# An LSTM with a residual: the sums of a step in two banks by halves of the features, matmuls of 256 columns

## The reference

```python
xW = einsum('ntd,dg->ntg', x, Wx) + b          # x: (32, 512, 512), Wx: (512, 2048)
def step(carry, xw_t):                          # 512 steps, batch 32, 512 features
    a = xw_t + prev_h @ Wh                      # Wh: (512, 2048)
    i, f, o = sigmoid(a[:, :3 * 512]) in thirds
    g = tanh(a[:, 3 * 512:])
    next_c = f * prev_c + i * g
    next_h = o * tanh(next_c)
return x + hs                                   # all hidden states, plus x
```

## Time and profile before

| | |
|---|---|
| median of 3 runs | 2726.16 us (2726.15 to 2726.85) |
| the profiled execution | 2726.29 us |
| its span, first to last instruction | 2724.5 us |
| matmuls, and as many weight loads | 49152 |
| mean granted clock of TensorE | 0.989 |

### The profile page before, as it was taken

One profiled execution on the slowest core, in us unless ns is written; L12 is line 12 of the kernel. 1 busy time (PEld: TensorE's weight loads), 2 busy tenths in 40 slices (PEclk: granted clock), 3 DMA queues, 4 the chain that ended last, 5 costly groups with the idle time before them and its releaser, 6 DMA issues.

```text
span 2724.5 us, 121148 instructions
## 1 busy us (share of the span) xinstructions
PE 2671.2 (98%) x49152; PEld 1387.0 (51%) x49152; DVE 1929.8 (71%) x8121; ACT 1245.7 (46%) x3722; POOL 45.9 (2%) x134
## 2 busy tenths in 40 slices
PE   3999999999999999999999999999999999999998
PEld 0455555555555555555555555555555555555554
DVE  6777777777777777777777777777777777777776
ACT  3444444444444444444444444444444444444444
POOL 0000000000000000000000000000000000000000
PEclk6999999999999999999999999999999999999999
DMA  6111111111111111111111111111111111111111
GB/s 144 37 43 35 38 38 40 35 39 42 35 38 38 40 35 39 42 35 38 38 39 35 39 42 35 39 38 39 35 39 42 35 39 39 38 35 39 42 36 26
DMA packets 223520, 109.94 MB, mean 40 GB/s; under 512 B 25216, under 2 KB 222464, under 8 KB 222464
## 3 DMA queue, kind: packets, MB, share of 16 engines
q1 hardware_dynamic: 223488, 109.48, 15.7%
HBM read 75.83 MB, written 33.55 MB: 40 GB/s over the span
## 4 chain that ended last, share of the span: by engine, by line
PE 97%; issue 1%; DVE 1%; DMA 1%; SPq 0%; ACT 0%; POOL 0%; DVEq 0%; POOLq 0%
PE Z L244 97%; DMA wx_raw<-in_Wx 1%; DVE wh_lo L435 0%; SPq L213 0%; SPq L200 0%; DVE wmax L417 0%; SPq L208 0%; DVE h_hi L475 0%; ACT tanh_c L356 0%; POOL wmax_all L537 0%; DVE xmax L396 0%; DVE x_lo L381 0%; DVE zs L407 0%; DVE c L490 0%; DVE scales L410 0%
## 5 line engine op out<-in xcount | busy, mean ns | idle before, releaser
L350 ACT ACTIVATE act<-Z,scales 128x192 f32<-128x192 f32 x1022 | 430.9, 422 | 1159.5 <-PE Z L244 1159.5
L244 PE MATMUL Z<-wx_hi,x_hi 128*32 128x512 f16 x8176 | 807.7, 379 | 9.3 <-DVE x_lo L381 9.3
L244 PE MATMUL Z<-wh_hi,hT_hi 128*32 128x512 f16 x8176 | 808.1, 379 | 8.0 <-DVE hT_hi L480 8.0
L244 PE MATMUL Z<-wh_lo,hT_hi 128*32 128x512 f16 x8176 | 808.1, 379 | 0.0
L244 PE MATMUL Z<-wx_hi,x_lo 128*32 128x512 f16 x8176 | 807.6, 379 | 0.0
L244 PE MATMUL Z<-wx_lo,x_hi 128*32 128x512 f16 x8176 | 807.6, 379 | 0.0
L244 PE MATMUL Z<-wh_hi,hT_lo 128*32 128x512 f16 x8176 | 533.1, 379 | 0.0
L486 DVE TENSOR_TENSOR fc<-act,c 128x64 f32<-128x64 f32 x512 | 115.3, 225 | 570.2 <-ACT act L350 570.2
L356 ACT ACTIVATE tanh_c<-c 128x64 f32<-128x64 f32 x1024 | 262.3, 256 | 269.7 <-DVE c L497 249.2
L475 DVE SCALAR_TENSOR_TENSOR h_hi<-act,scales,tanh_c 128x64 f16<-128x64 f32 x1024 | 291.3, 285 | 113.1 <-ACT tanh_c L356 86.3
L327 ACT ACTIVATE Z<-bias_bc,scales 128x512 f32<-128x512 f32 x511 | 344.6, 674 | 0.0
(11 more groups left out here) (50 smaller groups left out, 1286.1 us busy)
## 6 DMA issues: line engine op xcount, KB each, us to landing
x_in<-in_x SPq DMA_DIRECT2D x512, 64.0 KB, 2.0
x_res<-in_x SPq DMA_DIRECT2D x512, 64.0 KB, 2.1
out_y<-y SPq DMA_DIRECT2D x512, 64.0 KB, 1.7
wx_raw<-in_Wx SPq DMA_DIRECT2D x16, 256.0 KB, 8.8
wh_raw<-in_Wh SPq DMA_DIRECT2D x16, 256.0 KB, 19.0
bias_bc<-in_bias SPq DMA_DIRECT2D x4, 64.0 KB, 2.0
h_in<-in_h SPq DMA_DIRECT2D x4, 16.0 KB, 13.8
```

The lines of the kernel that those rows point to most:

```text
L244: return nc.tensor.matmul(bank[L * j:L * j + B, :], lhsT, rhs, start=False, stop=last, skip_group_check=True)
L350: nc.scalar.activation(half_gates(act, a)[:, 0:3], half_gates(Z[s], a)[:, 0:3], ACT.Sigmoid, scale=scale).then_inc(sig_done, 1)
```

## The change

A step's Z now takes two banks, one for each half of the features (a = 0, 1), with 256 columns in each: four gates of 64 features. Steps t and t+2 share a pair of banks, side by side in each bank. Every matmul of 512 columns becomes two of 256, with the same stationary operand loaded for each. The weights, `act` and the bias are laid out by halves (tile, half, gate, 64). In the recurrent part the low part of h comes last as before, but now all chunks for half 0 and then all for half 1, with a `z_done` after each; ScalarE waits for each half by itself. The bias is loaded by eight DMAs, the low parts of the weights are cut by gate and no longer by tile.

```diff
-        def bank(name):
-            return ctx.enter_context(nc.psum_tensor(name, [P, 512], F32))
+        def bank_pair(name):
+            return ctx.enter_context(nc.psum_tensor(name, [P, 2, 512], F32))
...
-        Z = [bank(f"Z{s}") for s in range(TB)]
+
+        Z = [bank_pair(f"Z{q}") for q in range(2)]
...
+        HW = ZW // 2
...
+        def gate(tile, a, g, n=1):
+            return tile[:, a * HW + g * HC:a * HW + (g + n) * HC]
+
+        def both_halves(tile, g):
+            return tile.rearrange("p (a g c) -> p g a c", a=2, g=4)[:, g]
+
+        def z_half(s, a, g=0, n=4):
+            at = s // 2 * HW
+            return Z[s % 2][:, a, at + g * HC:at + (g + n) * HC]
+
+        def by_half(w, j, a):
+            at = j * C + a * HC
+            return w.rearrange("p (g c) -> p g c", g=4)[:, :, at:at + HC]
+
+        def by_halves(w):
+            return w.rearrange("p (g k c) -> p k g c", g=4, c=HC)
+
+        def as_halves(w):
+            return w.rearrange("p (k g c) -> p k g c", g=4, c=HC)
+
+        def halves_of_gate(w, g):
+            return w.rearrange("p (k g c) -> p g k c", g=4, c=HC)[:, g]
+
+        def gate_by_halves(w, g):
+            return w[:, g * NJ * C:(g + 1) * NJ * C].rearrange("p (k c) -> p k c", c=HC)
...
             for j in range(NJ):
-                sp.dma_start(bias_bc[L * j:L * j + B].rearrange("p (g c) -> p g c", g=4),
-                             bias_view[j].partition_broadcast(B)).then_inc(bias_loaded, 16)
+                for a in range(2):
+                    sp.dma_start(bias_bc[L * j:L * j + B, a * HW:(a + 1) * HW].rearrange("p (g c) -> p g c", g=4),
+                                 bias_view[j, :, a * HC:(a + 1) * HC].partition_broadcast(B)).then_inc(bias_loaded, 16)
...
-            def add(bank, j, lhsT, rhs, last=False):
-
-                return nc.tensor.matmul(bank[L * j:L * j + B, :], lhsT, rhs, start=False, stop=last, skip_group_check=True)
+            def add(s, a, j, lhsT, rhs, last=False):
+
+                return nc.tensor.matmul(z_half(s, a)[L * j:L * j + B], lhsT, rhs, start=False, stop=last, skip_group_check=True)
...
-            for s in range(TB):
-                for j in range(NJ):
-                    mm = nc.tensor.matmul(Z[s][L * j:L * j + B, :], x_T[:, 0, 0, :],
-                                          x_in[:, 0].rearrange("p t c -> p (t c)"), start=True, stop=True)
-                mm.then_inc(banks_opened, 1)
+            for q in range(2):
+                for a in range(2):
+                    for j in range(NJ):
+                        mm = nc.tensor.matmul(Z[q][L * j:L * j + B, a], x_T[:, 0, 0, :],
+                                              x_in[:, 0].rearrange("p t c -> p (t c)"), start=True, stop=True)
+                    mm.then_inc(banks_opened, 1)
...
-                raw = by_tile(wx_raw[:, ch])
-                for j in range(NJ):
-                    add(Z[0], j, x_T[:, ch, 0, :], raw[:, j])
+                for a in range(2):
+                    for j in range(NJ):
+                        add(0, a, j, x_T[:, ch, 0, :], by_half(wx_raw[:, ch], j, a))
...
+            def columns(w, ch, j, a):
+                return w[:, ch, j * ZW + a * HW:j * ZW + (a + 1) * HW]
...
                     for xp, wp in ((x_hi, wx_hi), (x_hi, wx_lo), (x_lo, wx_hi)):
+                        for a in range(2):
+                            for j in range(NJ):
+                                mm = add(s, a, j, xp[:, r, ch, s * B:(s + 1) * B], columns(wp, ch, j, a))
+                mm.then_inc(xpart_done, 1)
+
+            def recurrent_part(t, s):
+                for ch in range(NCH):
+                    if ch % 2 == 0:
+                        pe.wait_ge(hT_hi_done, 2 * t - 1 + ch // 2)
+                    for w in (wh_hi, wh_lo):
+                        for a in range(2):
+                            for j in range(NJ):
+                                add(s, a, j, hT_hi[:, ch, :], columns(w, ch, j, a))
+                pe.wait_ge(hT_lo_done, t)
+
+                for a in range(2):
+                    for ch in range(NCH):
                         for j in range(NJ):
-                            mm = add(Z[s], j, xp[:, r, ch, s * B:(s + 1) * B], wp[:, ch, j * ZW:(j + 1) * ZW])
-                mm.then_inc(xpart_done, 1)
-
-            def recurrent_part(t, s):
-                for part, ht in enumerate((hT_hi, hT_lo)):
-                    for ch in range(NCH):
-                        if part == 0 and ch % 2 == 0:
-                            pe.wait_ge(hT_hi_done, 2 * t - 1 + ch // 2)
-                        if part == 1 and ch == 0:
-                            pe.wait_ge(hT_lo_done, t)
-                        for w in ((wh_hi, wh_lo) if part == 0 else (wh_hi,)):
-                            for j in range(NJ):
-                                mm = add(Z[s], j, ht[:, ch, :], w[:, ch, j * ZW:(j + 1) * ZW], part == 1 and ch == NCH - 1)
-                mm.then_inc(z_done, 1)
+                            mm = add(s, a, j, hT_lo[:, ch, :], columns(wh_hi, ch, j, a), ch == NCH - 1)
+                    mm.then_inc(z_done, 1)
...
-                nc.scalar.activation(Z[s][:, :], bias_bc[:, :], ACT.Copy, scale=scale).then_inc(bias_placed, 1)
-
-            sc.wait_ge(bias_loaded, 16 * NJ)
-            sc.wait_ge(banks_opened, TB)
+                at = s // 2 * HW
+                nc.scalar.activation(Z[s % 2][:, :, at:at + HW], bias_bc[:, :].rearrange("p (a w) -> p a w", a=2),
+                                     ACT.Copy, scale=scale).then_inc(bias_placed, 1)
+
+            sc.wait_ge(bias_loaded, 2 * 16 * NJ)
+            sc.wait_ge(banks_opened, 4)
...
-                    sc.wait_ge(z_done, t + 1)
                     for a in range(2):
-                        nc.scalar.activation(half_gates(act, a)[:, 0:3], half_gates(Z[s], a)[:, 0:3],
+                        sc.wait_ge(z_done, 2 * t + 1 + a)
+                        nc.scalar.activation(gate(act, a, 0, 3), z_half(s, a, 0, 3),
                                              ACT.Sigmoid, scale=scale).then_inc(sig_done, 1)
-                        nc.scalar.activation(half_gates(act, a)[:, 3], half_gates(Z[s], a)[:, 3],
+                        nc.scalar.activation(gate(act, a, 3), z_half(s, a, 3, 1),
                                              ACT.Tanh, scale=scale).then_inc(tanh_g_done, 1)
...
-                for j in range(NJ):
-                    cut = nc.vector.scalar_tensor_tensor(as_tiles(lo[:, ch])[:, j], by_tile(raw[:, ch])[:, j],
-                                                         w_scale[:, k:k + 1].bitcast(F32), as_tiles(hi[:, ch])[:, j],
+                for g in range(4):
+                    cut = nc.vector.scalar_tensor_tensor(halves_of_gate(lo[:, ch], g), gate_by_halves(raw[:, ch], g),
+                                                         w_scale[:, k:k + 1].bitcast(F32), halves_of_gate(hi[:, ch], g),
                                                          ALU.mult, ALU.subtract)
...
-                nc.vector.tensor_tensor(h32[:, :], act[:, 2 * C:3 * C], tanh_c[:, :], ALU.mult).then_inc(h32_done, 1)
+                nc.vector.tensor_tensor(h32[:, :].rearrange("p (a c) -> p a c", a=2), both_halves(act, 2),
+                                        tanh_c[:, :].rearrange("p (a c) -> p a c", a=2), ALU.mult).then_inc(h32_done, 1)
```

More of the change, by code:

```diff
@@ L220, in _ @@
             sp.wait_ge(x_turned, 1)
-            sp.wait_ge(banks_opened, TB)
+            sp.wait_ge(banks_opened, 4)
             load_x(2, 0)
@@ L333, in _ @@
             for ch in range(NCH):
-                nc.scalar.activation(as_tiles(wx_hi[:, ch]), by_tile(wx_raw[:, ch]), ACT.Copy,
+                nc.scalar.activation(as_halves(wx_hi[:, ch]), by_halves(wx_raw[:, ch]), ACT.Copy,
                                      scale=w_scale[:, 0:1].bitcast(F32)).then_inc(wx_hi_cut, 1)
@@ L474, in high_part_of_h @@
                 v.wait_ge(tanh_c_done, 2 * t + 1 + a)
-                nc.vector.scalar_tensor_tensor(half(h_hi, a), half_gates(act, a)[:, 2], h_scale(q), half(tanh_c, a),
+                nc.vector.scalar_tensor_tensor(half(h_hi, a), gate(act, a, 2), h_scale(q), half(tanh_c, a),
                                                ALU.mult, ALU.mult).then_inc(h_hi_done, 1)
@@ L485, in step @@
                 v.wait_ge(sig_done, 2 * t + 1)
-                nc.vector.tensor_tensor(half(fc, 0), half_gates(act, 0)[:, 1], half(c, 0), ALU.mult)
+                nc.vector.tensor_tensor(half(fc, 0), gate(act, 0, 1), half(c, 0), ALU.mult)
                 v.wait_ge(tanh_g_done, 2 * t + 1)
-                nc.vector.tensor_tensor(half(ig, 0), half_gates(act, 0)[:, 0], half_gates(act, 0)[:, 3], ALU.mult).then_inc(ig_done, 1)
+                nc.vector.tensor_tensor(half(ig, 0), gate(act, 0, 0), gate(act, 0, 3), ALU.mult).then_inc(ig_done, 1)
                 v.wait_ge(ig_done, 2 * t + 1)
@@ L491, in step @@
                 v.wait_ge(sig_done, 2 * t + 2)
```

(4 more changed lines are left out.)

13 lines of the change are left out of this document (3 added, 10 removed).

## The result

The changed kernel takes 3363.7 us (3358.4 to 3369.6, 4 runs) against 2726.4 us: ratio 1.234 (95% interval 1.231 to 1.237), 637 us slower. Forecast were 2938 us and 2755 to 3110; the direction was right, the size was not.

What follows compares the result with a forecast made beforehand. TensorE alone was taken to bound the kernel: 2724.5 + 30.7 (matmuls) + 1.9 (start) - 0.4 (order by half) + 180 (fetch misses at branches) = 2936.7 us of span, forecast 2938 us, range 2755 to 3110.

Steps and rivals of the forecast that it cites:

- What bounds the kernel: Whole kernel: TensorE alone sets the end; the chain through ScalarE and VectorE is hidden, TensorE busy 2671.2 of 2724.5 us.
- The matmuls: TensorE's steps: 48 groups of 109.2 ns, a step 5.24 us instead of 5.18, +30.7 us over 511 steps.
- The loads don't bound: TensorE's groups: a group's four loads can follow closer than 0.11 us, so they do not set its time.
- The rival in which they set the group: TensorE's groups: loads make a group 113 ns, +125 instead of +30.7 us; 2852 us without misses, 3032 with; chance 4%.
- the one in which alternating banks save the 2.5 ns: TensorE's groups: the fixed 2.5 ns vanish between different banks, a step 5.12 us, 2697 us in all; chance 2%.
- The order by half: Low part of the recurrent matmuls: earlier release of half 0 gains nothing in the steps, -0.4 us after the last.
- The start: SP's queue before the loop: four more bias DMAs, issued 0.47 us apart, delay Wx by +1.9 us.
- Thirteen blocks do not fit; a miss at each of 60 branches: TensorE's loop: the body of 12.1 blocks is fetched anew every pass, stalling at each backward branch, +180 us.
- the price of a miss: TensorE's backward branch: a fetch takes 3.0 us (bounds 2.4 and 6.9); stalls of 2.2 and 0.8 us a pass.
- the second rival: TensorE's loop: fetch in sequence becomes the bound, 3330 us, or the clock falls at each stall, 3040 us; chance 10%.
- the fetch in sequence: TensorE's loop: blocks fetched one after another; at 4 us a fetch each is 0.5 us late, +390 us; forecast counted nothing.
- the clock: TensorE's loop: falls to half after a stall, 1.7 us lost at each of 60 branches, +100 us; forecast counted nothing.

Runs made afterwards that it cites:

- a_resident: The changed kernel with TensorE's loop body of one block of 4 steps instead of two, x cut step by step: 2761.2 us, ratio 1.013.
- b_resident: The kernel before the change with TensorE's loop body of one block of 4 steps, x cut step by step: 2726.4 us, ratio 1.0001.
- a_res_plain: a_resident with the order by half undone, both halves of a step released together at the end: 2762.5 us.
- a_slot0: The changed kernel with the head of TensorE's loop placed at the first instruction of a fetch block: 3283.9 us, ratio 1.203.
- b_body4: The kernel before the change with TensorE's loop body lengthened to four blocks (16 steps, 12.1 fetch blocks), 512-column matmuls kept: 2819.8 us, ratio 1.034.
- a_28groups: The changed kernel's layout, but one bank a step and 512-column matmuls except for h's low part; loop body 7.1 fetch blocks: 2938.0 us, ratio 1.080.
- a_hint: The changed kernel with a branch hint at the head of TensorE's loop, meant to fetch the branch target's block ahead: 3263.4 us, ratio 1.197.

## Why the prediction was wrong

Point by point, with what was measured for each term.

- *What bounds the kernel*: right. TensorE waited for the chain once, before and after.
- *The matmuls, +30.7 us*: right. Groups of 109.2 ns, steps of 5.24 us; `a_resident` against `b_resident` is +34.8 us, which holds this term, the start and the tail.
- *The loads don't bound*: right, they are busy 2450 of 2450 us in `a_resident` and cost nothing. The rival in which they set the group fell, and so did the one in which alternating banks save the 2.5 ns.
- *The order by half, -0.4 us, at the end only*: right in kind, 0.6 us in the profile of `a_resident` against `a_res_plain`.
- *The start, +1.9 us*: the last Wx issue ends the queue's chain at 15.24 instead of 13.35, the first recurrent matmul of `a_resident` starts 2.1 us later than that of `b_resident`.
- *Thirteen blocks do not fit; a miss at each of 60 branches*: right. 887 packets, and the loss vanishes with a body that fits.
- **The first step that failed is the price of a miss**: "I take 3.0, near the lower end". From the branch to the next matmul it was 3.7 us in the pass shown (3.6 on average), of which 1.03 were before the packet, 1.05 the packet, and 1.6 after it. The lower bound of 2.4 us ended with the packet's last byte, and I gave the part behind it 0.6 us. The matmuls still queued covered 0.6 us and not 0.8, so the first gap cost 3.1 us instead of 2.2. For the second I took half of 1.6 us, between a next block asked for late and one asked for together; `a_slot0` shows that it is asked for late, and the gap cost 2.3. The mechanism at the branch was right, only larger: 5.4 us a pass and 324 us in all instead of 180. That lies inside the term's own bounds (84 to 348; the lower should read 60 x 1.6 = 96, since 2.4 - 0.8 is 1.6). With it alone the forecast would have been 3082 us, inside the range.
- **What took the time out of the range are two terms that the sum had at nothing**, both named in the second rival at 10%. The first is the fetch in sequence. With 3.0 us a fetch is shorter than the 3.49 us that a block lasts, and costs nothing; with 3.8 us it is longer. Against this I had held that "fetch and transfer would have to take 1.6 us beyond the packet". They do take about that: 1.6 us at the branch and some 1.4 in sequence. It costs 2.3 us a pass, 136 us in the loop. The rival's 0.5 us a block were too many twice: the distance is 3.8 and not 4 us, which leaves 0.3 a block or 3.7 a pass, and after a branch the blocks last longer at half clock.
- The second is the clock: I held 8 us of idle time against stalls of 3. But it fell in all 60 passes, in 33 of them before the second gap had begun: 6.7 us of every pass at 0.50, and 2.3 us a pass lost, 138 us in all. In `b_body4`, with gaps of 2.2 and 0.8 us, it fell in 2 passes of 28.

Together, for the profiled execution, whose span is 641.8 us longer: 30.7 + 2.1 - 0.6 for matmuls, start and end, 324 + 136 + 138 in the loop, and 10.5 us of such gaps in the blocks written out before and after it make 640.7. The rival's 3330 us was nearer than the forecast, but by luck: its condition priced the sequence alone, at 390 us where 136 were measured, and the stalls at 180; the clock, which it had as an alternative to the sequence, came on top.

Open: why the hint fails with the head at the start of a block, and how much of the 3.8 us other traffic makes in general. What decides whether the clock falls stays open too: one gap of 3.1 us did it in 14 of 60 passes, one of 3.7 with smaller ones ahead of it in 54 of 60, two of 1.4 and 2.4 with 0.7 us between in 41 of 60 (`a_28groups`, `a_slot0`, `a_hint`; starts of groups).

## What to carry to other kernels

Before splitting instructions in a loop, count what the body holds (here TensorE ran freely with 6.1 blocks of 256 instructions and refetched everything with 7.1), and compare the time that a block lasts with the 3.8 us from packet to packet. Here a hint at the loop's head saved nearly all where a block lasted 6.9 us, and a sixth of the loss where it lasted 3.49; there only the smaller body helped. Nothing between the two was tried. Where a threshold, here 3.49 us, lies inside the bounds of a price, the cases on its two sides are forecasts of their own.

## What was not expected of the hardware

A fetched block became usable only 1.6 us after its packet had ended, more than the packet itself took (1.05 us). A single gap of 3.1 us was enough to take the clock to 1.2 GHz in 14 of 60 passes of `a_28groups`; in the changed kernel, with a second gap of 2.2 us close behind, it stood there for 6.7 us of every pass. The hint took the first stall from 3.1 to 1.3 us with blocks of 3.49 us, and removed it with blocks of 6.9 us.
